# Layer 0's attention reordered: q ahead of k and V, relative sums by half axis, q.k terms ahead of one-hot terms

## The reference

```python
q, k, v = (qkv[0], qkv[1], qkv[2])
rel_h = jnp.einsum('bhwc,hkc->bhwk', qr, Rh)     # qr: q as heads x 16 x 16 x 16
rel_w = jnp.einsum('bhwc,wkc->bhwk', qr, Rw)
attn = jnp.einsum('bmd,bnd->bmn', q, k) * scale
attn = attn + rel_h[:, :, :, :, None] + rel_w[:, :, :, None, :]
p = jax.nn.softmax(attn, axis=-1)
o = jnp.einsum('bmn,bnd->bmd', p, v)
```

## Time and profile before

| | us |
|---|---|
| median of three runs | 223.0 |
| lowest, highest | 222.47, 224.26 |
| the profiled execution: its time | 224.36 |
| the profiled execution: its span, first to last instruction | 222.2 |
| PE busy in that span | 203.7 |
| DVE, ACT, POOL busy | 102.6, 64.0, 39.8 |

### The profile page before, as it was taken

One profiled execution on the slowest core, in us unless ns is written; L12 is line 12 of the kernel. 1 busy time (PEld: TensorE's weight loads), 2 busy tenths in 40 slices (PEclk: granted clock), 3 DMA queues, 4 the chain that ended last, 5 costly groups with the idle time before them and its releaser, 6 DMA issues.

```text
span 222.2 us, 5411 instructions
## 1 busy us (share of the span) xinstructions
PE 203.7 (92%) x2291; PEld 139.0 (63%) x2291; DVE 102.6 (46%) x285; ACT 64.0 (29%) x146; POOL 39.8 (18%) x64
## 2 busy tenths in 40 slices
PE   7899999989899999999999789988898999999951
PEld 7789987668545446545445488755686455757841
DVE  1432486847822331121111323878478579744411
ACT  2242057726222112222222323688241000000010
POOL 1512120003994000000000011200027950000000
PEclk9999999999999999999999889999999999999996
DMA  6999999953100000000000099999100000600001
GB/s 212 391 425 446 422 433 427 448 236 101 71 0 3 3 0 3 3 0 3 0 7 3 3 360 446 415 421 425 63 0 6 0 3 3 212 3 0 3 4 41
DMA packets 4991, 33.58 MB, mean 151 GB/s; under 512 B 664, under 2 KB 2144, under 8 KB 2656
## 3 DMA queue, kind: packets, MB, share of 16 engines
q1 hardware_dynamic: 4384, 32.37, 35.7%
q10 hardware_dynamic: 576, 0.79, 1.2%
HBM read 32.95 MB, written 0.20 MB: 149 GB/s over the span
## 4 chain that ended last, share of the span: by engine, by line
PE 79%; DVE 7%; issue 6%; ACT 2%; DMA 2%; POOL 2%; DVEq 0%; POOLq 0%; ACTq 0%
PE bank L1452 15%; PE bank L1396 13%; PE bank L1411 7%; PE bank L1092 7%; PE bank L1199 4%; PE bank L1371 4%; PE bank L1160 4%; PE bank L1184 3%; PE bank L1424 3%; PE bank L1314 3%; PE bank L1211 3%; PE bank L1124 3%; PE bank L1433 2%; DMA x<-x_dram 2%; PE bank L1362 1%
## 5 line engine op out<-in xcount | busy, mean ns | idle before, releaser
L1452 PE MATMUL bank<-w,scratch 128*32 128x192 f32 (+4 forms) x648 | 33.7, 329 | 0.7 <-ACT scratch L588 0.7
L1452 PEld LDWEIGHTS bank<-w,scratch 128*32 128x32 f32 (+4 forms) x648 | 19.5, 109 | 18.6 <-issue 10.5
L1396 PE MATMUL bank<-w,scratch 128*32 128x512 f32 (+3 forms) x332 | 31.0, 493 | 0.0
L1092 PE MATMUL bank<-ones 128*128 128x128 f32 x196 | 29.1, 306 | 1.8 <-POOL ones L500 1.4
L1092 PEld LDWEIGHTS bank<-ones 128*128 128x128 f32 x196 | 27.0, 217 | 3.0 <-POOL ones L500 1.4
L889 DVE TENSOR_TENSOR scratch<-scratch,bank 128x512 f32<-128x512 f32 (+1 forms) x12 | 7.9, 655 | 37.3 <-ACT scratch L597 37.3
L664 ACT ACTIVATE scratch<-bank,neg_max 128x256 f32<-128x256 f32 x48 | 19.7, 478 | 14.1 <-DVE neg_max L783 13.9
L508 POOL TENSOR_TENSOR rstd<-var_eps,minus_half 128x2 f32<-128x2 f32 x4 | 2.8, 708 | 107.9 <-DVE var_eps L734 107.9
L553 POOL TENSOR_SCALAR scratch<-const,place,gate 128x96 f32<-128x96 f32 x32 | 22.0, 699 | 0.5 <-issue 0.4
L1396 PEld LDWEIGHTS bank<-w,scratch 128*32 128x32 f32 x332 | 11.1, 109 | 11.9 <-issue 9.3
L1411 PE MATMUL bank<-w,scratch 64*32 64x512 f32 (+3 forms) x332 | 17.8, 497 | 0.0
(11 more groups left out here) (177 smaller groups left out, 261.4 us busy)
## 6 DMA issues: line engine op xcount, KB each, us to landing
w<-experts_dram SPq DMA_DIRECT2D x9, 1152.0 KB, 17.2
w<-experts_dram SPq DMA_DIRECT2D x1, 3624.0 KB, 42.2
w<-experts_dram SPq DMA_DIRECT2D x1, 3024.0 KB, 24.0
w<-experts_dram SPq DMA_DIRECT2D x1, 2496.0 KB, 34.1
w<-bias_slots_dram SPq DMA_DIRECT2D x1, 2304.0 KB
w<-experts_dram SPq DMA_DIRECT2D x1, 2016.0 KB, 28.8
w<-experts_dram SPq DMA_DIRECT2D x1, 1704.0 KB, 17.3
w<-experts_dram SPq DMA_DIRECT2D x1, 1416.0 KB, 12.6
```

The source lines that it names most:

```text
L1092: nc.tensor.matmul(bank[b][:, 0:P], ones[:], ones[:], start=True, stop=True)
L1396: nc.tensor.matmul(first_bank(m, which)[rows, to:to + wide], xe_hi[:, e, tokens_at(q, i)], w0[:, at:at + wide], start=col == 0, stop=False ...
L1452: last = nc.tensor.matmul(y_bank_of(layer, i)[UNIT * q:UNIT * (q + 1), 0:C], hT[0:k, col, UNIT * q:UNIT * (q + 1)], w0[0:k, at:at + C], st ...
```

## The change

Layer 1 keeps its order. In layer 0:

- PE does the lower part of k and q right behind the upper part; the router's sums and V come after.
- ACT makes all three `q_low` ahead of the three `kT`, DVE all three `q_parts` ahead of the three `k_hi`.
- `relative` no longer waits for the first `kT` at its start but for all three ahead of its second axis, writes other banks, and signals `rel_psum` after each half of an axis. ACT and DVE take a half when it is there; DVE's sums go half by half, three groups each.
- `rel_hi` is now written by ACT instead of DVE, in six pieces of [128, 8 x 16] (half axis by group) instead of three of [128, 256], and POOL's `rel_lo` likewise. `half_of` picks these pieces out of the token order, so that neighbouring elements of a piece lie 16 words apart. `rel_hi` shares memory with `q_low`, and the table's two parts have room of their own.
- For the first four heads all q.k products are issued ahead of all one-hot products, and only the latter wait for `rel_split`.
- POOL's splitting of the table waits until DVE has written `xnT`.
- The `keep_clock` calls ahead of `relative` and ahead of layer 0's scores are gone, and the first has 16 instead of 18.
- Of the products into a score bank only the first has `start`.

```diff
 # POOL
                 if n == 0:
+                    pool.wait_ge(xnT_vec, 1)
                     pool.wait_ge(rel_landed, 16)
                     nc.gpsimd.tensor_copy(rel_t_hi[:], rel_t[:]).then_inc(table_hi, 1)
...
-                        for g in range(HG):
-                            pool.wait_ge(rel_ready, 2 * (g + 1))
-                            pool.wait_ge(rel_rounded, g + 1)
-                            nc.gpsimd.tensor_tensor(rel_lo[:, g], relT[:, g], rel_hi[:, g].bitcast(F32), ALU.subtract).then_inc(rel_split, 1)
+                        for half in range(2):
+                            for g in range(HG):
+                                pool.wait_ge(rel_ready, HG * half + g + 1)
+                                pool.wait_ge(rel_rounded, HG * half + g + 1)
+                                nc.gpsimd.tensor_tensor(half_of(rel_lo, g, half), half_of(relT, g, half),
+                                                        half_of(rel_hi, g, half).bitcast(F32), ALU.subtract).then_inc(rel_split, 1)
...
+        def half_of(lines, g, half):
+
+            return lines[:, g, :].rearrange("p (r c) -> p c r", c=GRID)[:, 8 * half:8 * half + 8]
 # ACT
+                    for half in range(2):
+                        for g in range(HG):
+                            act.wait_ge(rel_ready, HG * half + g + 1)
+                            nc.scalar.copy(half_of(rel_hi, g, half), half_of(relT, g, half)).then_inc(rel_rounded, 1)
 # DVE
-                    dve.wait_ge(rel_psum, 2)
                     dve.wait_ge(rel_half, 2)
-                    for g in range(HG):
-                        for half, b in enumerate(REL_BANKS[1]):
+                    for half, b in enumerate(REL_BANKS[1]):
+                        dve.wait_ge(rel_psum, 3 + half)
+                        for g in range(HG):
...
-                        dve.wait_ge(rel_ready, 2 * (g + 1))
-                        nc.vector.tensor_copy(rel_hi[:, g], relT[:, g]).then_inc(rel_rounded, 1)
 # PE
-                if layer == 0:
-                    pe.wait_ge(q_split, 1)
-                    keep_clock(KEEP_TURN, 2)
-                    relative()
-
                 pe.wait_ge(ones_set, 4)
                 if layer == 0:
-                    pe.wait_ge(k_ready, HG)
-                    keep_clock(KEEP_SCORES[0], 5)
+                    relative()
+                    pe.wait_ge(rel_half, 2)
+                    for pair in range(2):
+                        scores(0, pair, (0,))
+                    scores(0, 0, (1,))
+                    pe.wait_ge(rel_ready, 2 * HG)
+                    scores(0, 1, (1,))
```

More of the change, by code:

```diff
@@ L124, in metaformer_kernel @@
         parts = sb("parts", [6, HG, TOK], F32R)
-        q_low, q_parts, k_hi, k_lo, rel_hi, rel_lo = (parts[:, i] for i in range(6))
-        rel_t_hi, rel_t_lo = (part.rearrange("p g t -> p (g t)")[:, 0:2 * REL_W].rearrange("p (a c) -> p a c", a=2)
-                              for part in (rel_hi, rel_lo))
+        q_low, q_parts, k_hi, k_lo, rel_lo = (parts[:, i] for i in (0, 1, 2, 3, 5))
+        rel_hi = q_low
+        rel_parts = parts[:, 4].rearrange("p g t -> p (g t)")[:, 0:4 * REL_W].rearrange("p (b a c) -> p b a c", b=2, a=2)
+        rel_t_hi, rel_t_lo = rel_parts[:, 0], rel_parts[:, 1]
         scratch = sb("scratch", [SCRATCH])
@@ L645, in _ @@
                 if layer == 0:
-                    act.wait_ge(rel_psum, 1)
+                    for g in range(HG):
+                        keep_q_low(g)
+                    for g in range(HG):
+                        keep_k(g)
+                else:
+                    for g in range(HG):
+                        keep_q_low(g)
+                        keep_k(g)
+                if layer == 0:
                     for half in range(2):
+                        act.wait_ge(rel_psum, half + 1)
                         rows = relT[:].rearrange("p g (r c) -> p r g c", c=GRID)[:, 8 * half:8 * half + 8]
@@ L760, in attend @@
                                                    q_low[:, g].bitcast(F32), ALU.add, ALU.subtract).then_inc(q_split, 1)
+                if layer == 0:
+                    for g in range(HG):
+                        split_q(g)
+                    for g in range(HG):
+                        round_k(g)
+                else:
+                    for g in range(HG):
+                        round_k(g)
+                        split_q(g)
                 dve.wait_ge(v_psum, layer + 1)
@@ L1161, in relative, with scores @@
                                                     start=table is rel_t_hi, stop=table is rel_t_lo, skip_group_check=True)
-                    last.then_inc(rel_psum, 1)
-            def scores(layer, pair):
+                        if i % 8 == 7:
+                            last.then_inc(rel_psum, 1)
+            def scores(layer, pair, parts_of=(0, 1)):
                 heads = (2 * pair, 2 * pair + 1)
                 g = heads[0] // HB
-                pe.wait_ge(q_split, HG * layer + g + 1)
-                pe.wait_ge(k_rounded, HG * layer + g + 1)
-                pe.wait_ge(k_split, HG * layer + g + 1)
-                if layer == 0:
-                    pe.wait_ge(rel_split, g + 1)
+                if 0 in parts_of:
+                    pe.wait_ge(q_split, HG * layer + g + 1)
+                    pe.wait_ge(k_rounded, HG * layer + g + 1)
+                    pe.wait_ge(k_split, HG * layer + g + 1)
+                if layer == 0 and 1 in parts_of:
+                    pe.wait_ge(rel_split, HG + g + 1)
                 for h in heads:
@@ L1175, in scores @@
                         pe.wait_ge(probs_ready, TT * (layer * HEADS + h - HB + 1))
-                terms = [(q_parts, k_hi), (q_parts, k_lo)]
+                terms = [(0, q_parts, k_hi), (0, q_parts, k_lo)]
                 if layer == 0:
-                    terms += [(rel_hi, None), (rel_lo, None)]
+                    terms += [(1, rel_hi, None), (1, rel_lo, None)]
                 for t in range(TT):
-                    for i, (left, right) in enumerate(terms):
+                    for i, (part, left, right) in enumerate(terms):
+                        if part not in parts_of:
+                            continue
                         for h in heads:
```

54 lines of the change are left out of this document (30 added, 24 removed).

## The result

The changed kernel took 221.05 us (median of 9 runs), the kernel before 223.75 us beside it (9 runs): ratio 0.9886, 95% interval 0.9851 to 0.9920, a gain of 2.7 us. The profiled execution took 219.9 us, with a span of 217.7.

A forecast was written before the change was run, and what follows sets the result against it. PE, busy 92% of the span, and its waits bound the kernel, with all hanging on layer 0's first maximum. Gains 0.58 + 1.10 + 0.94 + 0.89 = 3.51 us took the 223.0 median to 219.5, range 217.9 to 221.8.

The forecast's parts named there:

- Step 1: Layer 0's norm: POOL waits and fewer ones run, so L745 takes 0.35 instead of 0.95 us; gain 0.58 us.
- Step 2: Layer 0's projections: V's and the router's products move behind the lower half of q; gain 1.10 us.
- Step 3: Splitting q ahead of k on ACT and DVE: relative products start at 14.70; this step gains 0.94 us.
- Step 4: From relative products to first maximum: half axes, ACT casts and q.k products first; maximum at 25.00, gain 0.89 us.
- first rival: Spread pieces dearer on POOL, over 0.65 us each, delay the one-hot products: 220.3 us at 0.85, 221.7 at 1.20; 15%.
- rule of the Trainium skill: SBUF port runs at full rate only over adjacent word pairs; POOL's spread piece would grow to about 0.83 us.
- low end: Both pieces, ACT's and POOL's, at lower bounds (gain 4.0) and layer 1's slow-clock stretch of 1.1 us missing: 217.9 us.
- the loss on their account: Slower than before: four POOL pieces at 1.52 us or more, held up by DVE's sums; 223.6 us at 1.68; 5%.
- a norm that doesn't change: Layer 0's norm: L745 stays at 0.95 us for another reason; gain 2.9, 220.1 us; 7%.
- A slower clock in the attention: Without the removed ones PE idles and one half-clock stretch costs 1.1 us or a little more: 220.6 to 221; 8%.
- Lost later: The gain is lost to a wait in the experts: 222 to 223 us; 3%.

The follow-up runs named there:

- k and q in turns: Changed kernel with ACT and DVE taking k and q of each group in turn again, PE's order kept: 222.3 us, ratio to before 0.9953.
- V first: Changed kernel with V's and the router's upper products back ahead of the lower half of q: 222.9 us, ratio to before 0.9955.
- the gap's variant: Changed kernel with ones in PE's idle gap ahead of its one-hot products, and six instead of four behind them: 221.18 us, ratio to before 0.9881.
- five more instructions: Changed kernel with ones at the seam of the layers, plus five small fills at the head of DVE's list: 220.65 us, ratio to before 0.9870.

## Why the prediction was right

The forecast was 219.5 us with a range of 217.9 to 221.8, and 3.51 us of gain; measured were 221.05 and 2.7. The side and the mechanism were right, the gain was 0.7 to 0.8 too large. 221.05 lies in the range, but not in the 219.0 to 220.0 that the forecast gave 62%. Position by position:

| | before | forecast | after | gain, forecast | gain, measured |
|---|---|---|---|---|---|
| first projection | 9.54 | 8.96 | 8.94 | 0.58 | 0.60 |
| first `q_low` | 14.27 | 12.59 | 12.56 | 1.68 | 1.71 |
| relative products | 17.32 | 14.70 | 15.02 | 2.62 | 2.30 |
| first product behind POOL's wait (before q.k, after one-hot) | 27.29 | 24.27 | 24.60 | 3.02 | 2.69 |
| first maximum | 28.51 | 25.00 | 25.37 | 3.51 | 3.14 |
| experts | 60.29 | 56.78 | 57.41 | 3.51 | 2.88 |

**Step 1** came out to the hundredth in the profiled execution: L769 at 0.34 beside L745's 0.95, and the ones out of the way at 7.33. To the hundredth was luck. The forecast said that the ones must be out of the way too, and had 32 of them end near 7.5; that holds in this execution, but they ended at 6.8 in the profile with k and q in turns and at 8.1 in the one without POOL's wait, by when the clock rises (last section). So the 0.58 isn't there in every execution.

**Step 2** was right for q: V's 1.10 left the way to the first `q_low`, which is 0.03 from the forecast, and undoing it put the split 1.09 later. That the products moved into time in which PE waits anyway was not right: the chain after runs through them to the relative products.

**Step 3** is the term that was mis-sized, 0.6 for 0.94. Its first half was right: the last `q_parts` ends at 14.56, with 0.12 of hand-over 14.68, as worked out. What failed is the sentence on PE's own list, "near 14.7 by their pitch": it took the pitch from the order before. After the lower half of k and q come the router's sums, V's upper and V's lower part, and in this order the same products take longer. The last of them, first with V first, then in the changed kernel:

```profile
14.18 0.49 PE L1179 MATMUL bank<-att_lo,xnT 64*128 64x192 f32 x4
```

```profile
14.49 0.59 PE L1181 MATMUL bank<-att_lo,xnT 64*128 64x192 f32 x4
```

With V first the list ends at 14.67, 5.75 behind its first projection (8.92), as it did before (9.54, and L1142 ended at 15.29); in the new order it ends at 15.08, 6.14 behind 8.94. So 14.7 would have held for the old order. Some 0.2 of the 0.4 is at the router's sums (0.54 in the chain after, 0.35 in the earlier trace rows); why the order matters isn't shown. Taking these sums away moved the start to 14.73.

**Step 4** was right to 0.05 in sum (0.84 measured, 0.89 forecast) and in its parts: POOL's piece 0.62 (six in 3.73; 0.645 as a mean of overlapping records), ACT's 0.42 for 0.40, POOL the one that PE waits for last. POOL's first three pieces end at 23.82 in the chain and the fourth starts at 23.91, so POOL's own list and the path through ACT are level, as the forecast had it (23.41 and 23.51): at 0.65 a piece it was at the edge of the first rival. The surcharge for spread elements, taken as 0.14 from L777, is 0.19, on a piece of 0.45 in runs of eight instead of 0.48. The Trainium skill, GPSIMD Engine Reference, section 7, puts it, for kernels of the engine's own cores, at half as much again per element for reads in larger steps than 8 bytes; the measured 0.645 to 0.453 is 1.42 times for the whole piece. The rule of the Trainium skill that the forecast weighed (Vector Engine (DVE) Microarchitecture Reference, section 5.2) gave 0.83 for the piece, as an estimate, and the trace disagrees: that rule's 0.19 for 128 columns is the surcharge itself here, and not a factor on POOL's slower column.

**Behind the maximum** I held that all lists are the same and nothing is lost. 0.25 was lost, in the pause of DVE: from the maximum to the pause and from there to the experts the two traces agree to 0.02. An equal list behind a shorter one was not an equal list.

**The level of the time.** 219.5 was set against a median of 223.0, and by its time that run was one without the slow stretch at the seam; the kernel after mostly has it. For it to be absent was the forecast's low end, and it was left out of the middle. With the stretch removed in both, the forecast would be 222.66 - 3.51 = 219.15, and 219.87 was measured: 0.32 of step 3, 0.25 of the pause, 0.05 of step 4, and 0.1 that the runs can't tell.

**The rivals.** Dear pieces on POOL, the loss on their account, and a norm that doesn't change fell with the rows above, the first of them narrowly. A slower clock in the attention didn't come in the changed kernel's profile, but it lay close: three of four kernels with one part undone had it there, and the one run of the changed kernel at 0.976 may have. The argument against it misread a row: a gap of 0.7 us is not shorter than the 0.45 in which PE is idle from 50 to 52 us, and the gap came to 1.05. "Lost later" was right in kind and small.

## What to carry to other kernels

When work is taken off the path of one engine, add up the list of every engine that arrives at the same point, with each product in its new place, and don't take its length from the old order; here the engine that was thought to wait arrived 0.3 us after the one it was to wait for. Work that can go into a gap of TensorE may earn twice, by its own time and by the clock behind the gap. And before 1% is read from a median, sort the runs by granted clock: a single slow stretch that costs 1.2 us, by the mean clocks present in half the runs of one kernel and nearly all of the other, is as large as half of what is to be measured.

## What was not expected of the hardware

- Half clock follows a stand of PE, but not each time. The changed kernel at the seam is busy 0.96 of the two microseconds at 120 us in the profile without a slow stretch, and the gap's variant is busy 1.05 in the profile with one. In the attention, V first and the kernel with five more instructions have the same busy time and another clock. Why the changed kernel, by its mean clocks, has a slow stretch in eight of nine runs and the kernel before in 33 of 61 isn't settled.
- A place in DVE's list cost 0.25 us in ten kernels, and moved out of the path with the count of instructions ahead.
- The ones at the start run at half clock at first, and when that ends differs. Records of the changed kernel in two microseconds of the start:

```profile
5.00:6.00 1.00, 1.00 (x7) 1.00 (x7) 0.86 (x5) 0.00 (x0) 0.00 (x0) 1.00 1.08 362
6.00:7.00 1.00, 1.00 (x11) 1.00 (x11) 0.19 (x2) 0.00 (x0) 0.72 (x1) 1.00 1.10 409
```

  In the kernel before, the ones at the seam start every 0.213 us at a granted clock of 0.50 (six in the microsecond of the earlier trace rows) and every 0.112 at 1.00. At the start it is 0.213, too, until the change, and 0.112 from there. The 1.00 in the first row is no reading: the trace's record of the granted clock begins only at the change, at 5.85 us here, at 4.73 in the profile with k and q in turns and at 7.46 without POOL's wait. The ones end at 7.33, 6.79 and 8.10 in this order; in the kernel before with the wait alone the change comes at 7.52, and its 36 records end at 8.58.
- Elements 16 words apart cost POOL 1.42 times and ACT 1.42 times (422 to 298 ns) what runs of eight cost.
